# Value products of a windowed attention on 64 by 64 array tiles, with P transposed and copied as it is

## The reference

```python
x = x + 0.5 * _L0_ffn_ref(_layernorm(x), ...)   # the stack: 6 layers of attention and FFN
x = x + _L0_attn_ref(_layernorm(x), ...)        # Mamba
x = x + 0.5 * _L0_ffn_ref(_layernorm(x), ...)   # the stack again

def local_attention(q, k, v):                   # 16 heads of 64, windows of 32 tokens
    bq = q.reshape(b, h, nw, w, d)              # w = 32
    bk2, bv2 = look(bk), look(bv)               # each window sees itself and the one before: 64 keys
    sim = einsum('bhwie,bhwje->bhwij', bq, bk2) * 8
    attn = softmax(where(mask, -max, sim))      # P: 32 queries by 64 keys for each head and window
    out = einsum('bhwij,bhwje->bhwie', attn, bv2)
```

## Time and profile before

| | |
|---|---|
| median of 3 runs | 3331.24 us (3329.32 to 3331.4) |
| profiled execution: span of the core's instructions | 3329.5 us |
| profiled execution's own time beside its span | not noted apart; the span lies 1.74 us below the median of the runs |
| PE, PEld busy | 3179.2 us (95%), 2524.1 us (76%) |
| DVE, ACT, POOL busy | 2793.2 us (84%), 2503.3 us (75%), 2435.9 us (73%) |
| mean granted clock of TensorE | 0.993 |

### The profile page before, as it was taken

The page is one execution under the profiler, slowest core; times in us unless marked ns, Lnnn a source line. Parts: engine busy times, 40 slices in busy tenths (PEclk is TensorE's granted clock), DMA queues, the critical chain, the costliest instruction groups (busy, mean ns, idle before and its releaser), DMA issues.

```text
span 3329.5 us, 120453 instructions
## 1 busy us (share of the span) xinstructions
PE 3179.2 (95%) x51630; PEld 2524.1 (76%) x51630; DVE 2793.2 (84%) x3207; ACT 2503.3 (75%) x3160; POOL 2435.9 (73%) x1229
## 2 busy tenths in 40 slices
PE   7999999999999999998888999999999999999999
PEld 5888888888887887875333778788788888788777
DVE  7888888888888888877999888888888888888886
ACT  5777777777777777777676777777777777778776
POOL 6777777777777776672999768768768768768664
PEclk8999999999999999999999999999999999999999
DMA  3333333233233232221000323323323323323222
GB/s 120 84 75 87 74 82 89 71 86 88 67 90 85 67 90 65 65 72 38 30 0 0 97 67 81 86 69 86 89 70 82 95 67 80 96 65 85 69 65 69
DMA packets 142299, 245.22 MB, mean 74 GB/s; under 512 B 32397, under 2 KB 34638, under 8 KB 141774
## 3 DMA queue, kind: packets, MB, share of 16 engines
q1 hardware_dynamic: 141774, 237.51, 28.0%
HBM read 35.01 MB, written 1.05 MB: 11 GB/s over the span
## 4 chain that ended last, share of the span: by engine, by line
PE 79%; DVE 7%; issue 7%; POOL 4%; ACT 3%; DMA 0%; SPq 0%; DVEq 0%; POOLq 0%; ACTq 0%
PE PS L282 15%; PE PS L408 11%; PE PS L428 8%; PE PS L214 8%; PE PS L216 7%; PE PS L215 7%; PE PS L349 6%; PE PS L550 4%; ACT ARENA L955 3%; PE PS L492 2%; PE PS L494 2%; PE PS L493 2%; POOL ARENA L1868 2%; PE PS L451 2%; DVE ARENA L1681 2%
## 5 line engine op out<-in xcount | busy, mean ns | idle before, releaser
L1760 POOL TENSOR_TENSOR ARENA<-ARENA,RN 128x1024 f32<-128x1024 f32 x192 | 365.6, 1904 | 456.0 <-ACT RN L945 456.0
L282 PE MATMUL PS<-C,ARENA 128*128 128x128 f32 x4608 | 615.0, 277 | 42.9 <-ACT ARENA L955 16.4
L1752 POOL TENSOR_TENSOR ARENA<-ARENA 128x1024 f32<-128x1024 f32 x192 | 468.3, 2439 | 228.9 <-DVE ARENA L1331 228.1
L282 PEld LDWEIGHTS PS<-C,ARENA 128*128 128x128 f32 x4608 | 512.9, 141 | 119.7 <-issue 76.4
L214 PE MATMUL PS<-WL,XH 128*128 128x512 f32 x1152 | 489.7, 425 | 7.3 <-POOL XL L1719 4.0
L1010 ACT ACTIVATE ARENA<-PS 64x1024 f32<-64x1024 f32 x384 | 390.5, 1017 | 98.0 <-PE PS L282 94.6
L1746 POOL TENSOR_TENSOR ARENA<-ARENA 128x1024 f32<-128x1024 f32 x192 | 457.3, 2382 | 7.0 <-DVE ARENA L1313 7.0
L216 PE MATMUL PS<-WH,XH 128*128 128x512 f32 x1152 | 454.2, 394 | 0.0
L215 PE MATMUL PS<-WH,XL 128*128 128x512 f32 x1152 | 452.1, 392 | 0.0
L408 PE MATMUL PS<-ARENA 128*64 128x64 f32 x12288 | 403.7, 224 | 42.0 <-DVE ARENA L1371 26.0
L408 PEld LDWEIGHTS PS<-ARENA 128*64 128x64 f32 x12288 | 378.7, 139 | 77.1 <-issue 77.1
(11 more groups left out here) (160 smaller groups left out, 6476.1 us busy)
## 6 DMA issues: line engine op xcount, KB each, us to landing
ARENA<-ARENA SPq DMA_DIRECT2D x1152, 128.0 KB
ARENA<-ARENA SPq DMA_DIRECT2D x768, 64.0 KB
ARENA<-in_wqkv SPq DMA_DIRECT2D x36, 512.0 KB, 5.1
ARENA<-in_wo SPq DMA_DIRECT2D x12, 512.0 KB, 3.9
ARENA<-in_w SPq DMA_DIRECT2D x12, 341.0 KB, 3.5
ARENA<-in_w SPq DMA_DIRECT2D x12, 192.0 KB, 3.9
X<-in_xT SPq DMA_DIRECT2D x4, 256.0 KB, 6.0
out<-X SPq DMA_DIRECT2D x1, 768.0 KB, 3.6
```

The costliest lines, as they stand in the source:

```text
L282: last = nc.tensor.transpose(PS[:, slot, 128 * j:128 * j + 128], src[:, 128 * j:128 * j + 128], ident)
L1752: nc.gpsimd.tensor_tensor(KN[n % 2], KN[n % 2], T2, ALU.add).then_inc(k_add, 1)
```

## The change

It does five things. `PTS` shrinks to 1024 columns (the 1024 behind it are left unused, so that all other buffers stay where they were). `p_evacuate` copies the transposed P as it is, 128 partitions by 1024 columns in one pass. `value_products` issues, for each pair and window, two matmuls in place of one: for `par` 0 and 1 apart, with 64 rows and 64 columns of weights, and 32 moving columns. The array tile is given by `par` (rows) and `side` (columns), and the two values of `par` write to different banks of slot 3. The output columns come to lie in another order, which `out_products` follows by its choice of weights (`i`). The clearing of `PTS` and its semaphore go; in their place ACT waits at tile 0 for `m_out`, a count of the Mamba layer's last products.

```diff
-        PTS = take(2048)
+        PTS = take(1024)
+        take(1024)
...
             def value_products(n):
-                pt = PTS.rearrange("p (h w x) -> p h w x", h=8, w=4)
+                pt = heads(PTS, 8)
                 v2 = V2[n % 2].rearrange("p (w h d) -> p w h d", w=4, h=8)
                 for m in range(4):
                     for win in range(4):
-                        for side in range(2):
-                            hp, col = 2 * m + side, 32 * win
-                            out = PS[64 * side:64 * side + 64, 3, 256 * m:256 * m + 256]
-                            last = nc.tensor.matmul(
-                                out.rearrange("p (a q) -> p a q", a=2)[:, :, col:col + 32], v2[:, win, hp, :],
-                                pt[:, hp, win, :], start=True, stop=True, skip_group_check=True)
+                        for par in range(2):
+                            for side in range(2):
+                                hp, a, b, col = 2 * m + side, 64 * par, 64 * par + 64, 32 * win
+                                o = 512 * par + 128 * m + col
+                                last = nc.tensor.matmul(
+                                    PS[64 * side:64 * side + 64, 3, o:o + 32], v2[a:b, win, hp, :],
+                                    pt[a:b, hp, col:col + 32], start=True, stop=True, skip_group_check=True)
...
             def out_products(n, bank):
                 w = WO[n // NT % 2]
                 for j in range(8):
-                    last = nc.tensor.matmul(PSB[:, bank, 0:128], w[:, 128 * j:128 * j + 128], OTS[:, 128 * j:128 * j + 128],
+                    i = 2 * (j % 4) + j // 4
+                    last = nc.tensor.matmul(PSB[:, bank, 0:128], w[:, 128 * i:128 * i + 128], OTS[:, 128 * j:128 * j + 128],
...
                 if n >= 1:
                     act.wait_ge(pv_done, n0 + n)
                 else:
-                    act.wait_ge(zero_set, r + 1)
-                blocks = PTS.rearrange("p (b a q) -> p b a q", a=2, q=32)
-                for par in range(2):
-                    a, b = 64 * par, 64 * par + 64
-                    last = act.activation(blocks[a:b, :, par, :], PS[a:b, slot, :].rearrange("p (b q) -> p b q", q=32), ACT.Copy)
-                last.then_inc(PT_ev, 1)
+                    act.wait_ge(m_out, 4 * r)
+                act.activation(PTS, PS[:, slot, :], ACT.Copy).then_inc(PT_ev, 1)
...
-                nc.gpsimd.memset(PTS, 0.0).then_inc(zero_set, 1)
...
-                if s == 17 + 3 and r == 1:
-                    pool.wait_ge(m_out, 4)
-                    nc.gpsimd.memset(PTS, 0.0).then_inc(zero_set, 1)
```

More of the change, by code:

```diff
@@ L147, in build @@
         v2_in = [sem(f"v2_in{i}") for i in range(2)]
-        eps_set, pad_set, zero_set, masks_set, edge_set, tab_set = (sem(n) for n in (
-            "eps_set", "pad_set", "zero_set", "masks_set", "edge_set", "tab_set"))
+        eps_set, pad_set, masks_set, edge_set, tab_set = (sem(n) for n in (
+            "eps_set", "pad_set", "masks_set", "edge_set", "tab_set"))
         i_mu, i_sq, i_var, i_ln, i_rs, i_done = (sem("i_" + n) for n in (
```

## The result

| | before | after |
|---|---|---|
| median of the runs | 3330.93 us (3329.32 to 3331.40, 4 runs) | 3395.93 us (3390.27 to 3410.59, 4 runs) |
| ratio | | 1.020 (1.018 to 1.022) |
| the profiled execution: span | 3329.5 us | 3393.1 us (its own time 3394.9) |
| mean granted clock | 0.993 | 0.984 |

What follows compares the result with a forecast made beforehand. PE was taken to bound the kernel, busy 95% of the span. Span 3329.5 - 2 (value products) = 3327.5 us, other terms nothing; with 1.7 us from span to median, 3329 us, range 3306 to 3380.

Steps and rivals of the forecast that it cites:

- Value products, their pace: PE's value products: 32 rounds of 59 ns a tile, bound by the 64-column weight load, 1.89 us as before; 2 us off.
- check value of 197 ns: Value products at L410: their mean time in the changed profile was to fall from 224 ns to about 197.
- The copy of P: ACT's copy of transposed P: one pass for two, 194 us less ACT time, all hidden, costed at nothing.
- Clearing, semaphores, order of the output: POOL's clearing of PTS, ACT's new wait and the output's weight addresses: at most 1.8 us once, taken as 0.
- PE fetches 24,576 more pairs of instructions: PE's instruction fetch: the added instructions were stated, with no time given for them in the sum.
- the feed binds: Value products: PE's sequencer feeds pairs at 16.7 ns, 0.25 us more a tile, 48 us, 3379 us; chance 0.12.
- No pair of array tiles excludes the other: Denies the rival at L408 that only two array tiles overlap: 1.89 us more a tile, 3694 us; chance 0.10.
- the stream does not set the pace: Denies the rival that value products run at the stream's pace, 9.8 ns each: 123 us off, 3208 us; chance 0.09.

Runs made afterwards that it cites:

- e10: The kernel before with only the one-pass copy of transposed P, its products not matching the value layout: 3328.3 us, ratio 0.999 to 1.001.
- e8: The changed kernel with every tile's value products issued twice: 4205.1 us, ratio to the kernel before 1.260 to 1.265.
- e13: The kernel before with both halves of a tile's score products given together: 3298.4 us, ratio 0.988 to 0.991.
- e14: The changed kernel with both halves of a tile's score products given together: 3431.0 us, ratio to the kernel before 1.029 to 1.032.
- e7: The kernel before with every tile's value products issued twice: 3689.4 us, ratio 1.106 to 1.110.
- e12: The changed kernel without projection weight loads for layers 1 to 5, which use the first layer's: 3378.1 us, ratio to the kernel before 1.013 to 1.016.
- e5: The changed kernel with 47 small products in front and one Q transpose given twice every eighth tile, holding packet ends in place: 3392.9 us.
- e6: The changed kernel with 6 small products in front and one Q transpose given twice every eighth tile: 3409.8 us.
- e4: The changed kernel with the copy of transposed P again in two passes of 64 partitions: 3401.6 us, ratio to the kernel before 1.019 to 1.023.

## Why the prediction was wrong

- **Value products, their pace (right).** A group without a stop still takes its 1.87 us: loads 136 ns (139 before), 121 products in 1.99 us. With half the columns streamed and the pace unchanged, the stream is not what binds it; that it is the load of 64 columns fits, but no run changed the load alone. My check value of 197 ns for the products' mean was wrong: it is 221, since a record holds its latency and its wait behind the load, not only its columns. The group's start-to-start time is what counts, and that held.
- **The copy of P (right).** 195.2 us in 192 passes; ACT's busy time fell by 192.5, and L937 waits 203.9 us where L934 waited 51.7. e10 puts its worth at about 2 us, inside the measurement.
- **Clearing, semaphores, order of the output (no sign of a cost).** Not tried alone. e8 repeats only the products and grows the loss as supply says.
- **"PE fetches 24,576 more pairs of instructions" (the step that failed).** The number was wrong, 12,288 pairs; and the sum has no term for it, which puts it at nothing without a reason. I asked whether PE can issue a pair in 14.8 ns, and the score products said yes. I did not ask how long such a row may be. A row of 64 pairs is half a packet, and what stands around it gives the next packet time to come. A row of 128 is a whole one, gone in 1.87 us, where a packet that is late comes 2.2 us or more after its transfer has begun. Measured: 44 of the 64 us are stalls at packet ends (45.9 - 1.7), and 13.6 of the other 19 are the up products, part of which ran at the lower clock behind the long stalls.
- **The row that I had.** The page of the kernel before counts 415 packets of 16 KB for its instructions. With the span, 3329.5 / 415 = 8.0 us a packet on average, against 1.87 us for a packet of value products. That quotient does not say how short a packet may be, but it names the resource whose rate the change doubles for 1.87 us. The same trace holds the limit: in the kernel before no packet was entered less than 2.5 us after its transfer began. A page would have helped too: the Trainium skill, Advanced Engine Details and Errata, section ISA Cache, gives an instruction cache of 32 KB, 128 on TensorE, in lines of 16 KB, 256 instructions, and says that there are only two lines. The packets and the places of the stalls agree with the line of 256 instructions. The transfers agree with two lines, one in use and one on its way; no run here tells how large the cache is.
- **The rival "the feed binds" (right name, wrong mechanism).** I gave it 3379 us and 0.12, as a uniformly slower pace from 14.8 ns on. The pace between stops did not change; the cost is whole stops, at places set by the count of all instructions before, and it depends on what else the DMA queues carry.
- **The other rivals.** No pair of array tiles excludes the other (3694), and the stream does not set the pace (3208).
- **The range** ended at 3380 because the feed rival had one value. Two bounds for it, from nothing to one stop per tile of about a microsecond, would have reached 3520 (3329 + 192, with what is known now).

## What to carry to other kernels

Count the instructions of a short, dense row on an engine, not only their time: divide them by the instructions per packet that the page gives (bytes by packets of the instruction queue), and compare the packet's duration with those that pass without a stop in the same trace, and with the time from the beginning of a packet's transfer to its first instruction. Giving the same work in twice the instructions at equal time is not free once some 200 of them stand in a row; here it costs 2%. And a visit to array tiles has an entrance and an exit of about 0.3 us together, so join what needs them, and look what the joined row does at packet ends: in e13 joining gained 32 us over the kernel before, in e14 it lost 35 to the changed kernel.

## What was unexpected in the hardware

- Instructions come in packets of 256, and PE often stops at a packet's end when about 200 instructions in front of it took about 1.4 us; 128 instructions in 1.87 us (before), or 256 in 3.7 us (e7), do it little harm (3 and 10 stalls). At each such stop PE goes on 2.2 to 3.2 us after the late packet's transfer began. Most stops last 0.3 to 2 us; the five longest of the changed kernel, 3.3 to 4.2 us, stand beside loads of the projections' weights and are gone without them (e12).
- A stop of nearly 4 us costs more than itself: behind the one at 821.7 us the granted clock was at 1.2 GHz (0.50) for 3.4 us.
- Moving all packet ends by 82 instructions, with 41 small products more in the faster of the two and nothing else changed, moves the time by 17 us (e5 against e6). Two versions of a kernel whose instruction counts differ can differ by that much for this reason alone.
- The saving that the change was made of, ACT's 192.5 us, did nothing for the time that can be measured: 2 us alone (e10), and within the spread when taken back (e4, 3401.6 against 3395.9).
